# Eight loads moved from the last stage into the stage before it, and other indices for the gathers of nodes without edges

## The reference

```
x = layernorm(x)                                 # M = 12500 nodes
h = (x @ W_gat).reshape(M, 4 heads, 4 experts)
e = leaky_relu(a_src[src] + a_dst[dst])          # 131072 router edges, and one loop for each node
alpha = softmax of e over the edges that end in one node
agg = segment_sum(h[src] * alpha, dst) + b_gat
scores = layernorm(agg).mean over heads          # one score for each node and expert
w = softmax of the two best scores, 0 for the other two experts
out = x_in + sum over e of w[e] * (gelu(x @ W1[e] + b1[e]) @ W2[e] + b2[e])
```

## Time and profile before

| | us |
|---|---|
| Median of three runs | 10,581.45 |
| Lowest and highest run | 10,565.86 and 10,588.97 |
| Span of the profiled execution, first to last instruction | 9,343.6 |
| Median less that span | 1,237.9 |

### The profile page before, as it was taken

How to read it: one execution, slowest core, us unless ns; L and a number is a source line. 1 busy time by engine, 2 the same in 40 slices (tenths; PEclk the granted TensorE clock), 3 DMA queues, 4 the chain that set the end, 5 groups by cost and what they waited for, 6 DMA issues and landing times. The chain is left out here.

```text
span 9343.6 us, 84677 instructions
## 1 busy us (share of the span) xinstructions
PE 7050.5 (75%) x22541; PEld 4069.0 (44%) x22541; DVE 6127.7 (66%) x17477; ACT 3442.0 (37%) x7552; POOL 5141.1 (55%) x5326
## 2 busy tenths in 40 slices
PE   1536666666668999999997577777777559999986
PEld 1422222322235655655556233333333346666655
DVE  9967777777786555555545688888888862333335
ACT  1324443443443333333334344444444452333324
POOL 0157777777761011001433777777777567777763
PEclk9868888888889999999998777777777759999998
DMA  3156667766661000000315676777777542222229
GB/s 122 66 171 218 219 221 222 222 218 219 219 207 42 19 28 28 19 28 30 26 23 141 207 223 223 222 223 226 221 222 223 186 132 60 69 67 69 69 78 317
DMA packets 664832, 1341.17 MB, mean 144 GB/s; under 512 B 202459, under 2 KB 400958, under 8 KB 663458
## 3 DMA queue, kind: packets, MB, share of 16 engines
q0 software_dynamic: 238688, 579.40, 24.2%
q1 hardware_dynamic: 399040, 730.71, 22.0%
q10 hardware_dynamic: 26626, 25.65, 0.8%
HBM read 711.27 MB, written 636.81 MB: 144 GB/s over the span
## 5 line engine op out<-in xcount | busy, mean ns | idle before, releaser
L1269 POOL DMA_INDIRECT g_acc<-htab,g1sm_src x1760 | 1687.1, 959 | 545.8 <-issue 488.0
L1269 POOL DMA_INDIRECT g_acc<-htab,g0sm_src x1740 | 1651.2, 949 | 540.7 <-issue 456.8
L1379 PE MATMUL g1sm_sump<-g_acc,g1sm_to 128*128 128x264 f32 x3520 | 1494.8, 529 | 435.2 <-DVE g_acc L1525 356.3
L1379 PE MATMUL g0sm_sump<-g_acc,g0sm_to 128*128 128x260 f32 x3520 | 1337.3, 476 | 354.5 <-DVE g_acc L1525 259.0
L1379 PEld LDWEIGHTS g1sm_sump<-g_acc,g1sm_to 128*128 128x128 f32 x3520 | 656.0, 232 | 1227.7 <-DVE g_acc L1525 838.1
L809 POOL DMA_INDIRECT re_rerows<-rtab,re_resrc x1024 | 1001.4, 978 | 312.0 <-issue 311.7
L1379 PEld LDWEIGHTS g0sm_sump<-g_acc,g0sm_to 128*128 128x128 f32 x3520 | 590.1, 210 | 1069.0 <-DVE g_acc L1525 727.3
L2409 DVE SCALAR_TENSOR_TENSOR g_acc<-f_yp,f_wgt,g_acc 128x256 f32<-128x256 f32 x784 | 342.5, 478 | 952.2 <-PE f_yp L2329 948.4
L2197 POOL DMA_DIRECT2D x<-g_acc x25 | 20.0, 800 | 1552.4 <-DVEq L2418 1399.6
L1548 DVE SCALAR_TENSOR_TENSOR g_acc<-g_acc,g1sm_side,g1sm_sump 128x264 f32<-128x264 f32 x1705 | 818.1, 480 | 0.3
L1548 DVE SCALAR_TENSOR_TENSOR g_acc<-g_acc,g0sm_side,g0sm_sump 128x260 f32<-128x260 f32 x1705 | 812.6, 477 | 0.3
(11 more groups left out here) (458 smaller groups left out, 9961.5 us busy)
## 6 DMA issues: line engine op xcount, KB each, us to landing
sums<-g_acc SPq DMA_DIRECT2D x440, 528.0 KB, 3.6
sums<-g_acc SPq DMA_DIRECT2D x440, 520.0 KB, 3.8
z<-k_arena SPq DMA_DIRECT2D x96, 512.0 KB
k_arena<-z SPq DMA_DIRECT2D x33, 1024.0 KB, 14.8
g_acc<-htab,g1sm_src POOLq DMA_INDIRECT x1760
g_acc<-htab,g0sm_src POOLq DMA_INDIRECT x1740
x<-g_acc POOLq DMA_DIRECT2D x48, 512.0 KB, 3.4
re_rerows<-rtab,re_resrc POOLq DMA_INDIRECT x1024
```

Source lines behind the costliest of these rows:

```text
L1269: nc.gpsimd.indirect_dma_start(slot[a][:, u, :], None, table, bass.IndirectOffsetOnAxis(ap=src[a][:, u:u + 1], axis=0)).then_inc(landed[a] ...
L1379: nc.tensor.matmul(sump[u % BANKS][:, 0:W], to[u // LOT % RING][:, u % LOT, :], slot[a][:, u, 0:W], start=True, stop=True).then_inc(summed, 1)
```

## The change

First, a function `first_outputs` issues the loads of the `z` of pairs 0 to 7, those whose buffers lie in `arena`, as the first thing that SyncE does in `finish`, ahead of the store of the last piece. `choose_and_sum` no longer issues these eight. `x` and `z` of a buffer get a semaphore each: TensorE waits for `z_in` alone, VectorE for both. Second, `endi` of a node without edges becomes the node's own number. GpSimd writes the node numbers into `endi` with an iota, and VectorE computes with four more instructions `own + has * (start + count - 1 - own)`.

```
@@ EdgeSums.split_keys, before endi is written
+        dve.wait_ge(self.named, 1)
+        link(copy(self.own[:, :], self.endi[:, :]))
+        link(tt(tmpn[:, :], tmpn[:, :], self.own[:, :], ALU.subtract))
+        link(tt(tmpn[:, :], tmpn[:, :], has[:, :], ALU.mult))
+        link(tt(tmpn[:, :], tmpn[:, :], self.own[:, :], ALU.add))
         link(ts(tmpn[:, :], tmpn[:, :], 0.0, None, ALU.max))
         link(copy(self.endi[:, :], tmpn[:, :]))
@@ EdgeSums.fetch
         nc.gpsimd.iota(self.base[:, :], [[0, 1]], base=0, channel_multiplier=self.cols).then_inc(self.numbered, 1)
+        nc.gpsimd.iota(self.endi[:, :], [[P, NB]], base=0, channel_multiplier=1).then_inc(self.named, 1)
@@ EdgeSums.finish
                 def _(sp):
+                    load_first(sp)
                     self.store(sp, NG, col, n)
@@ new
+def first_outputs(nc, c, z, arena):
+    width = 2 * z.shape[1]
+    held = arena.shape[1] // width
+    places = [arena[:, s * width:(s + 1) * width].rearrange("p (j f) -> p j f", j=2) for s in range(held)]
+    z_in = [c.sem(f"z_in{s}") for s in range(held)]
+    zv = z.rearrange("(b p) f -> p b f", p=P)
+
+    def load_first(sp):
+        for n in range(held):
+            sp.dma_start(places[n], zv[:, 2 * n:2 * n + 2, :]).then_inc(z_in[n], 16)
+
+    return places, z_in, load_first
@@ choose_and_sum
                     sp.dma_start(x[s][:, :, :], xv[:, 2 * n:2 * n + 2, :]).then_inc(x_in[s], 16)
-                    sp.dma_start(zs[s], zv[:, 2 * n:2 * n + 2, :]).then_inc(x_in[s], 16)
+                    if n >= early:
+                        sp.dma_start(zs[s], zv[:, 2 * n:2 * n + 2, :]).then_inc(z_in[s], 16)
...
-                    pe.wait_ge(x_in[s], 32 * (n // XS + 1))
+                    pe.wait_ge(z_in[s], 16 * (n // XS + 1))
...
-                    dve.wait_ge(x_in[s], 32 * (n // XS + 1))
+                    dve.wait_ge(x_in[s], 16 * (n // XS + 1))
+                    dve.wait_ge(z_in[s], 16 * (n // XS + 1))
```

More of the change, by code:

```diff
@@ L713, in __init__ @@
         self.first = c.sb("refirst", [P, cols])
-        self.tmpn = c.sb("retmpn", [P, NB])
+        self.tmpn, self.own = c.sb("retmpn", [P, NB]), c.sb("reown", [P, NB])
+        assert NB * P <= P * cols
         self.ad = c.sb("read", [P, most, H])
@@ L726, in __init__ @@
              "piece_done", "kept", "placed"))
+        self.named = c.sem("renamed")
         every = self.rows[:, :, :].rearrange("p c w -> p (c w)")
@@ L743, in keep_nodes @@
         act.wait_ge(self.moved, 1)
-    SPLIT = 22
+    SPLIT = 26
     def split_keys(self, dve):
@@ L886, in sums, with finish @@
         assert link.n == self.SUMS
-    def finish(self):
+    def finish(self, load_first):
         nc, K, H, W, D, X, NG = self.nc, self.K, self.H, self.W, self.D, self.X, self.NG
@@ L2655, in _, with choose_and_sum @@
                 step(NCH - 1, LAST, 0, NG - 1, NG // 2 - 1, 1)
-def choose_and_sum(nc, K, name, rsum, endi, has, H, NE, asn, adn, hn, bias, gamma, beta, xin, z, out, arena):
+def first_outputs(nc, c, z, arena):
[8 more added lines that the diff above has]
+    return places, z_in, load_first
+def choose_and_sum(nc, K, name, z_in, early, rsum, endi, has, H, NE, asn, adn, hn, bias, gamma, beta, xin, z, out, arena):
     F, X = H * NE, 2 * H + H * NE
@@ L2691, in choose_and_sum @@
         x_in = [c.sem(f"x_in{s}") for s in range(XS)]
+        z_in = z_in + [c.sem(f"z_in{s}") for s in range(early, XS)]
         stored = [c.sem(f"stored{s}") for s in range(YS)]
@@ L2956, in gnn_two_layers @@
             rsum = dram("rsum", (RE, C))
+            early, z_in, load_first = first_outputs(nc, r, z, arena)
             with Ctx(nc, "re") as e:
@@ L2960, in gnn_two_layers @@
                 expert_outputs(nc, K, "f1", xs[3], z, experts, edges, room)
-                edges.finish()
-            choose_and_sum(nc, K, "cs", rsum, endi, has, H, NE, asn, adn, hn, a[f + "b_gat"], a[f + "ln_gamma"],
+                edges.finish(load_first)
+            choose_and_sum(nc, K, "cs", z_in, len(early), rsum, endi, has, H, NE, asn, adn, hn, a[f + "b_gat"], a[f + "ln_gamma"],
                            a[f + "ln_beta"], xs[3], z, out, arena)
```

## The result

The changed kernel took 10,602.31 us (median of 20 runs, 10,579.67 to 10,640.4) beside 10,587.74 us for the kernel before on the same chip (20 runs, 10,562.77 to 10,622.43). The ratio is 1.0019, 95% interval 1.0011 to 1.0028: about 20 us slower, 12 to 30; the two medians lie 14.6 us apart. I had forecast 10,577 and a range to 10,598. The three runs that I reckoned from had a median of 10,581.45, the 20 runs of the same kernel 6.3 us more, and that part of the miss is the runs' own spread.

A forecast was written before the change was run, and what follows sets the result against it. It took TensorE's line of pairs' matmuls, with holes for choosing and a stall from costly gathers, as the bound. Indices -18.8 and early loads +14.0 gave -4.8 us: 10,581.45 to 10,577, range 10,556 to 10,598.

The forecast's parts named there:

- The step that failed: Span 9,343.6 us against median 10,581.45: the 1,237.9 us between were taken as outside the span and untouched.
- the term of the indices: Last stage, third part of pairs: without slow shared-row gathers it takes 43.5 us, not 62.3, a gain of 18.8 us.
- the third part would start about 100 us after the first gather: Sign in the last stage's profile: a start much earlier than 100 us after the first gather would prove the forecast wrong.
- The early loads: Last-piece stage: the store queues behind 8.39 MB of z, `rf_met` starts 14.0 us later, nothing is given back.
- The sum: Whole kernel: -18.8 for the indices plus 14.0 for the loads gives -4.8 us, hence 10,577.
- Making the indices: One iota and four VectorE instructions, about 1 us, covered by VectorE's idling: cost 0, or 1 us if uncovered.
- Not held back: Last-piece stage: the store overtakes the loads or they drain sooner, only the 18.8 gain remains: 10,563; chance 0.13.
- Transfers bound the whole stage: Last stage: all bytes and engine time saved count, 36.7 us faster after the loads' 14.0: 10,545; chance 0.10.
- Adjacent rows as slow as the shared one: Last stage: gather price stays at 0.92 us, no 18.8 gain, the 14.0 come on top: 10,595; chance 0.15.

The follow-up runs named there:

- e1: The kernel before, unchanged, profiled a second time: 9,344.95 us beside 9,346.1 (0.9999), span 9,347.4.
- e2: The new indices alone, without the early loads, against the kernel before: 9,325.23 us, ratio 0.9978.
- e8: The new indices alone, repeated on a second quick chip, against the kernel before at 9,343.23: 9,327.03 us, ratio 0.9981.
- e12: The new indices alone, on a slower chip, against the kernel before at 10,576.88: 10,574.18 us, ratio 0.9997.
- e3: The early loads alone, indices as before, against the kernel before: 9,358.58 us, ratio 1.0011.
- e9: The early loads alone, repeated on a second quick chip, against the kernel before at 9,343.23: 9,358.08 us, ratio 1.0016.
- e11: The early loads alone, indices as before, on a slower chip, against the kernel before at 10,576.88: 10,591.04 us, ratio 1.0013.
- e4: The changed kernel with the last piece's store issued ahead of the eight early loads; against the kernel before: 9,331.75 us, ratio 0.9985.
- e5: The changed kernel again, on another slower chip, against the kernel before at 10,586.54: 10,608.75 us, ratio 1.0018.
- e13: The kernel before without the gathers of blocks 64 to 97, zeros in their place, against the kernel before at 10,521.88: 10,468.53 us, ratio 0.9949.
- e14: New indices alone, VectorE waiting for all 98 gathers before its first choosing, against the kernel before at 10,521.88: 10,550.07 us, ratio 1.0031.
- e6: Changed kernel, store first, gathers of blocks 64 to 97 replaced by zeros, against the kernel before at 10,586.54: 10,566.47 us, ratio 0.9974.

## Why the prediction was wrong

**The step that failed** is the first: "The 1,237.9 us between them lie outside the span and nothing in the change bears on them, so I work out a difference in the span and add it to the median". They lie inside. In e1 and in every later profile, on either kind of chip, the span is about 2 us short of the time of its own execution, and the windows show that the difference grows where GpSimd has most to issue. What I worked out was true of another execution than the ones timed.

**With it falls the term of the indices.** The mechanism is real: gathers of one shared row held the engines, other rows ease them, and where the third part runs beside them it is worth 21 us in e2 and 16 in e8 (18.8 forecast, third part 43.84 for 43.5). On the 10,590 chips the third part begins 185 us after the first gather, behind all gathers, and there is no hole to close: e12 measured 0.9997, 2.7 us faster with bounds of 15 faster and 7 slower. The forecast that the third part would start about 100 us after the first gather failed with it, on the late side, while I had named only the early side as a danger.

**The early loads** were right. 12.3 to 12.6 us to the first gather in the profiles and 12.5, 15 and 14 in the times (e3, e9, e11), for 14.0. That the store queues behind them is shown by e4, that they give nothing back by the same run beside e2. I had the drain a little long, and what lies between `rf_met` and the first gather took 0.4 us less than before's 11.0.

**The sum** is then about +11 by the two halves on one 10,590 chip (14.2 less 2.7 in the medians), where the whole change measured +14.6 in the medians and +20 (12 to 30) by the ratio and, in e5, +22 in the medians (-1 to 38 by the interval). The intervals overlap; whether the halves together cost some us more is open. Between my -4.8 and +14.6 lie 19.4 us, and 16.1 of them are the term of the indices.

**Making the indices** cost nothing that can be seen: e12 is no slower than before.

**The rivals.** "Not held back" is out: `rf_met` came 13 us later in every trace with the loads in front. "Transfers bound the whole stage" is out: the loads saved there gave nothing in e3 or e11. "Adjacent rows as slow as the shared one" named the time best, 10,595, and for the wrong reason: their share was 4.6 and 4.1%. That its figure came near is luck. What happened on the timed chips, the gain absent because the third part is late, was none of my cases.

**What stays open.** Why a signal takes longer on one kind of chip while GpSimd issues indirect transfers, and what sets the two kinds apart, is not shown; that it goes with the gathers being issued is shown by e13 and e14. The change as a whole was not run on a 9,346 chip (its halves add up to 8 us faster on one such chip and 1 on the other, by the medians; argued only), nor e4's order alone on a 10,590 chip, and the kernel before has no trace from a 10,590 chip; e11 stands in for it.

**The better version** is the new indices without the early loads: 0.998 on one kind of chip and no change on the other. Leaving the 34 gathers out gave more where it ran (0.995), if it is known that these nodes have no edges.

## What to carry to other kernels

Compare the span of the profile with the median of the timed runs before anything else. In the later profiles here the two were within 25 us, in the first 1,238 apart. A difference like that means that the profile is of an execution unlike the ones timed, and every "beside" and "behind" read from it is in doubt. A saving that rests on two streams meeting, here the costly gathers and the third part, is worth only what their overlap is worth in the timed execution, so give the case that they do not meet a price. And before work is moved into an idle queue, look at the small transfer behind it for which someone waits: 8.39 MB in front of 144 KB cost 12.5 us, and putting the small one first halved that but did not undo it.

## What was unexpected of the hardware

- One kernel took 9,343 to 9,346 us on two chips and 10,522 to 10,587 on three. On the slower ones, in the stretches where GpSimd issued indirect transfers, most instructions of 0.17 us chained by semaphores started 1.41 us apart instead of 0.21, and an end of TensorE reached three engines 28 to 34 us late. It was over 9 us behind the last gather issued in e6, 12 in e14 and 16 in the trace after.
- So on those chips an indirect transfer costs other engines time though it moves little and nobody waits for it: 34 fewer made the last stage 35 us shorter.
- A gather of 128 rows of 96 bytes took 0.92 us of the 16 DMA engines when all rows were one row of DRAM, 0.05 when they were scattered and 0.07 when they were adjacent.
